# A delta-rule layer on raw keys and queries, its 32x32 systems solved as two 16x16 blocks and a corner made on TensorE

## What is computed

```python
y = b; y = y + w[:, i] * xp[:, i:i + L, :]     # short_conv: 4 taps, then silu on v, unit length on q and k
def step(S, inp):                              # per batch and head, S is 32 x 32
    q_t, k_t, v_t, b_t = inp
    pred = jnp.einsum('bhk,bhkv->bhv', k_t, S)
    S = S + b_t[..., None, None] * (k_t[..., None] * (v_t - pred)[..., None, :])
    o_t = jnp.einsum('bhk,bhkv->bhv', q_t, S)
```

## Time and profile before

| | us |
|---|---|
| median of 3 runs (lowest, highest) | 3324.48 (3321.13, 3328.08) |
| the profiled execution's own time | 3335.67 |
| its span | 3333.9 |
| stage one within it, first output step to last | 0 to about 1325 |
| busy, whole span: TensorE, VectorE, ScalarE, GpSimd | 2692.8, 2510.2, 1182.5, 620.9 |

### The profile page before, as it was taken

One profiled execution on the slowest core, in us unless ns is written; L12 is line 12 of the kernel. 1 busy time (PEld: TensorE's weight loads), 2 busy tenths in 40 slices (PEclk: granted clock), 3 DMA queues, 4 the chain that ended last, 5 costly groups with the idle time before them and its releaser, 6 DMA issues. The chain is left out here.

```text
span 3333.9 us, 88364 instructions
## 1 busy us (share of the span) xinstructions
PE 2692.8 (81%) x35334; PEld 1912.9 (57%) x35356; DVE 2510.2 (75%) x4464; ACT 1182.5 (35%) x2016; POOL 620.9 (19%) x800
## 2 busy tenths in 40 slices
PE   7577777777777755999999995697769999968987
PEld 5455655555555543677777763344456767646664
DVE  6888887888888872477777783887857787834887
ACT  5233333333333320122222221654446565521221
POOL 3232222333322221000000000002600000002343
PEclk9789888888888866999999997899989999988888
DMA  3000000010000101301111112545941212142231
GB/s 88 3 15 28 29 28 29 28 29 28 29 28 29 47 22 64 128 20 51 51 50 50 50 48 89 196 176 179 319 116 51 76 50 76 59 143 83 83 94 51
DMA packets 229643, 234.68 MB, mean 70 GB/s; under 512 B 24112, under 2 KB 157872, under 8 KB 229296
## 3 DMA queue, kind: packets, MB, share of 16 engines
q1 hardware_dynamic: 229296, 229.70, 21.6%
HBM read 136.84 MB, written 92.81 MB: 69 GB/s over the span
## 5 line engine op out<-in xcount | busy, mean ns | idle before, releaser
L1132 PE MATMUL ctxatt_banks<-ctxatt_xT,ctxatt_wq 128*128 128x256 f32 x1024 | 232.9, 381 | 2.9 <-ACT ctxatt_qT L1208 2.1
L1171 PE MATMUL ctxatt_banks<-ctxatt_wo,ctxatt_oT 128*128 128x512 f32 x512 | 230.8, 604 | 4.9 <-DVE ctxatt_norm_y L1277 4.9
L826 DVE TENSOR_TENSOR delta_a<-delta_t_sys 128x30 f32<-128x30 f32 (+14 forms) x480 | 223.3, 465 | 10.3
L849 DVE SCALAR_TENSOR_TENSOR delta_conv<-delta_line,delta_conv_w,delta_conv 128x256 f32<-128x256 f32 x384 | 206.9, 560 | 3.4 <-DVE delta_ss L772 2.1
L829 DVE TENSOR_TENSOR delta_t_sys<-delta_t_sys,delta_a 128x30 f32<-128x30 f32 (+14 forms) x480 | 200.2, 417 | 11.4
L1132 PEld LDWEIGHTS ctxatt_banks<-ctxatt_xT,ctxatt_wq 128*128 128x128 f32 x1024 | 190.0, 191 | 28.7 <-ACT ctxatt_qT L1208 3.3
L393 POOL TENSOR_TENSOR delta_conv<-delta_conv,delta_product 128x256 f32<-128x256 f32 x192 | 148.7, 784 | 263.0 <-ACT delta_product L658 262.7
L508 PE MATMUL delta_banks<-delta_states,delta_kqT 32*32 32x32 f32 x4096 | 60.3, 209 | 154.0 <-DVE delta_states L868 95.2
L489 PE MATMUL delta_banks<-delta_xT,delta_wkT 128*128 128x256 f32 x512 | 135.9, 416 | 43.3 <-ACT delta_beta_T L640 35.8
L656 ACT ACTIVATE delta_conv<-delta_line,delta_conv_b,delta_conv_w 128x256 f32<-128x256 f32 x192 | 115.3, 601 | 153.3 <-POOL delta_conv L393 141.6
L1171 PEld LDWEIGHTS ctxatt_banks<-ctxatt_wo,ctxatt_oT 128*128 128x128 f32 x512 | 96.4, 193 | 117.0 <-issue 110.5
(11 more groups left out here) (328 smaller groups left out, 6728.3 us busy)
## 6 DMA issues: line engine op xcount, KB each, us to landing
h<-ffn_hid SPq DMA_DIRECT2D x66, 256.0 KB, 2.0
ffn_hid<-h SPq DMA_DIRECT2D x6, 1536.0 KB, 13.0
wkv_xT<-xT SPq DMA_DIRECT2D x64, 129.0 KB, 2.8
delta_xT<-xT SPq DMA_DIRECT2D x64, 128.0 KB, 3.0
delta_x<-x SPq DMA_DIRECT2D x16, 512.0 KB, 3.6
xT<-delta_newT SPq DMA_DIRECT2D x64, 128.0 KB, 2.8
x<-delta_new SPq DMA_DIRECT2D x16, 512.0 KB, 3.5
ctxatt_xT<-xT SPq DMA_DIRECT2D x64, 128.0 KB, 2.6
```

What stands on the lines that cost most here:

```text
L826: c.did(dve.tensor_tensor(terms, t_sys[:, j + 1:, j:j + 1].to_broadcast([P, rows, j]), t_sys[:, j:j + 1, 0:j].to_broadcast([P, rows, j]), ...
L849: c.did(dve.scalar_tensor_tensor(to, line[:, i, g, :, j:j + P], conv_w[:, i, g, j:j + 1], to, ALU.mult, ALU.add))
L1132: mm = pe.matmul(b_q[:, i * B * P:(i + 1) * B * P], wq[:, k, pair * P:(pair + 1) * P], xT_sb[:, n.parity, k], start=k == 0, stop=k == KB - 1)
L1171: mm = pe.matmul(b_o[:], oT[:, b, k, :], wo[:, k, :], start=k == 0, stop=k == PAIRS - 1)
```

## The change

Only stage one is edited (the class `ScaledNorm` moves up in the file; a later stage uses it as before).

- Keys and queries stay raw. `kqT` is a copy of the convolution's output by ScalarE (`keep_kq`), no longer turned back by VectorE. The norm of a key enters as `rate` = beta / norm squared (`rate_keys` on GpSimd), into the mask of K K' and into T; that of a query enters through the epsilon of the RMS norm (`q_norm`). `normalise` and `scale_v` are gone.
- All four taps are products on ScalarE, four instructions a projection after the first move (before two); GpSimd adds two of them for a whole third of the projections (`pair_taps`, 128x1024), VectorE adds the rest (`join`, six of 128x1024 a step). `tap` and `add_tap` are gone. silu is one instruction of ScalarE; beta is a tanh and an affine pass.
- A mask is one operation of 128x512 for keys and queries, four a step instead of eight of 128x256.
- The system of 32 is taken as [[T11, 0], [T21, T22]]. `substitute` makes T11 and T22 together, 28 operations instead of 60. Then T21 = T22 (A21 T11): `cross` on TensorE (128 calls of a 32x32 weight with 16 columns), `keep_corner` on ScalarE, `make_corner` on TensorE (128 calls more), `join_corner` on VectorE. `from_systems` has a second transpose (`inverse`). `cross` and `make_corner` use the two banks of `keys_keys`.
- The layer norm's scaling goes from VectorE (`norm.apply`) to ScalarE (`finish`); the outputs' RMS chain has one operation fewer.
- SP issues the stores of t4 ahead of the load of x for t2.
- The order on each list changes; TensorE's is shown in the diff. On GpSimd it is: `scale_t` (t2), `pair_taps` 2 (t1), history 0, `scale_outputs` (t3), `rate_keys` and `mask_beta` (t1), history 1 and 2, bias, `pair_taps` 0 and 1, the norm's root. On VectorE: RMS sum, `turn` 0 and 1, `miss` 0, RMS root, squares, `join_corner`, `join` 4, norms, `join` 5, `turn_outputs`, `turn_beta`, masks 0 and 1, `carry` 0, masks 2 and 3, `to_systems`, `miss` 1, then the 28 operations with the rest between them, `carry` 3, `from_systems`.

The core of the diff:

```diff
+                def pair_taps(n, i):
+                    wait(pool, taps_made, n, TAP_OPS, (i + 1) * MADE)
+                    two_taps, last = slot(n, i)[:, 1], slot(n, i)[:, 2]
+                    pool.tensor_tensor(two_taps, two_taps, last, ALU.add).then_inc(paired, 1)
+
+                def rate_keys(n):
+                    wait(pool, inverted, n, INVERT_OPS, INVERT_OPS)
+                    wait(pool, beta_turned, n, 1, 1)
+                    of_items = rate[:, n.parity].rearrange("p (g x) -> p g x", g=KB)
+                    by_item = beta[:, n.parity, :, 0:KB].rearrange("p x g -> p g x")
+                    pool.tensor_tensor(of_items, r[:, 0].rearrange("p (g x) -> p g x", g=KB), by_item, ALU.mult).then_inc(rated, 1)
 
                 def mask_beta(n):
-                    wait(pool, beta_turned, n, 1, 1)
-                    wait(pool, solved, n, SOLVE_OPS, 0)
+                    wait(pool, rated, n, 1, 1)
+                    wait(pool, masked, n, MASK_OPS, 0)
                     if isinstance(n.index, int) and n.index == 0:
                         pool.wait_ge(loaded, 16 * LOADS)
+                        pool.tensor_copy(weights_kq[:, :, 1], masks[:, 1].unsqueeze(1).to_broadcast([P, ITEMS, DD]))
                     earlier = masks[:, 0].unsqueeze(1).to_broadcast([P, ITEMS, DD])
-                    pool.tensor_tensor(by_group(a_sb[:]), by_group(earlier), beta_of(n), ALU.mult).then_inc(beta_masked, 1)
-
...
-                    pool.tensor_tensor(by_group(tT[:]), by_group(tT[:]), beta_of(n), ALU.mult).then_inc(t_scaled, 1)
+                    wait(pool, joined_corner, n, 1, 1)
+                    pool.tensor_tensor(tT[:], tT[:], rate_of(n), ALU.mult).then_inc(t_scaled, 1)
 
...
+                    if g < 2:
+                        wait(pe, masked, n, MASK_OPS, g - 1)
+                        if g == 1:
+                            wait(pe, joined_corner, n, 1, 0)
+                        else:
+                            wait(pe, corner_kept, n, 1, 0)
+                    else:
+                        wait(pe, masked, n, MASK_OPS, g - 1)
                     cols = b_kk[:, g % 2].rearrange("p (i x) -> p i x", i=QI)
                     pe.sem_inc(passed, 1)
                     for j in range(QI):
...
+                def cross(n):
+                    wait(pe, solved, n, SOLVE_OPS, SOLVE_OPS)
+                    cols = b_kk[:, 0].rearrange("p (i x) -> p i x", i=ITEMS)
+                    pe.sem_inc(passed, 1)
+                    for i in range(ITEMS):
+                        for h in heads():
+                            mm = pe.matmul(cols[h, i], masked_kq[h, n.parity, i, 0], tT[h, i, HALF_DD:], start=True, stop=True)
+                    mm.then_inc(crossed, 1)
+
+                def make_corner(n):
+                    wait(pe, corner_kept, n, 1, 1)
+                    cols = b_kk[:, 1].rearrange("p (i x) -> p i x", i=ITEMS)
+                    pe.sem_inc(passed, 1)
+                    for i in range(ITEMS):
+                        for h in heads():
+                            mm = pe.matmul(cols[h, i], inverse[h, i], corner[h, i], start=True, stop=True)
+                    mm.then_inc(corner_made, 1)
+
...
                             pe.matmul(cols[h, i], kqT[h, n.parity, 1, i], states[h, c, lane], start=True, stop=False)
-                            mm = pe.matmul(cols[h, i], pk[h, n.parity, i, 0], u[h, i], start=False, stop=True)
+                        for h in heads():
+                            mm = pe.matmul(cols[h, i], masked_kq[h, n.parity, i, 1], u[h, i], start=False, stop=True)
                     mm.then_inc(read, 1)
...
+                        cross(t2)
+                    if n:
                         project(n, 2)
                     if t2:
+                        make_corner(t2)
+                    if n:
+                        project(n, 3)
+                    if t1:
+                        keys_keys(t1, 0)
+                        keys_keys(t1, 1)
+                    if t2:
                         update(t2, 0)
                     if n:
-                        project(n, 3)
+                        project(n, 4)
                     if t2:
                         step_state(t2, 0)
+                    if t1:
+                        keys_keys(t1, 2)
+                    if t2:
                         outputs(t2, 0)
-                    if n:
-                        project(n, 4)
+                    if t1:
+                        keys_keys(t1, 3)
+                    if t2:
+                        predict(t2, 1)
+                    if n:
                         project(n, 5)
-                    if t1:
-                        keys_keys(t1, 0)
-                    if t2:
-                        predict(t2, 1)
-                    if t1:
-                        keys_keys(t1, 1)
-                        keys_keys(t1, 2)
-                        keys_keys(t1, 3)
-                    if n:
                         project(n, 6)
                     if t2:
                         update(t2, 1)
...
+                    wait(act, lined, n, len(GROUPS), p)
                     act.activation(conv[:, i, g].rearrange("p (b t) -> p b t", b=B), ln[:, :, 0:P], ACT.Identity,
-                                   bias=conv_b[:, i, g:g + 1], scale=conv_w[:, i, g, 0:1]).then_inc(started, 1)
-                    act.activation(product[:, p % PRODUCTS].rearrange("p (b t) -> p b t", b=B), ln[:, :, 1:1 + P], ACT.Identity,
-                                   scale=conv_w[:, i, g, 1:2]).then_inc(started, 1)
+                                   bias=conv_b[:, i, g:g + 1], scale=conv_w[:, i, g, 0:1]).then_inc(taps_made, 1)
+                    for j in range(1, TAPS):
+                        act.activation(slot(n, i)[:, j - 1, g].rearrange("p (b t) -> p b t", b=B), ln[:, :, j:j + P], ACT.Copy,
+                                       scale=conv_w[:, i, g, j:j + 1]).then_inc(taps_made, 1)
+
+                def keep_kq(n, i):
+                    wait(act, joined, n, JOIN_OPS, 2 * i + 2)
+                    wait(act, read, n, CHUNKS, -CHUNKS)
+                    act.activation(flat(kqT[:, n.parity, i]), conv[:, i].rearrange("p g n -> p (g n)"), ACT.Copy).then_inc(kq_kept, 1)
...
+                def keep_corner(n):
+                    wait(act, crossed, n, 1, 1)
+                    act.activation(flat(corner[:]), b_kk[:, 0], ACT.Copy).then_inc(corner_kept, 1)
+
...
+                def join(n, k):
+                    i = k // 2
+                    total = conv[:, i].rearrange("p g n -> p (g n)")
+                    c = Chain(dve, joined, n, JOIN_OPS)
+                    c.count = k
+                    if k % 2 == 0:
+                        wait(dve, taps_made, n, TAP_OPS, (i + 1) * MADE)
+                    else:
+                        c.settle()
+                        wait(dve, paired, n, 3, i + 1)
+                    c.did(dve.tensor_tensor(total, total, slot(n, i)[:, k % 2].rearrange("p g n -> p (g n)"), ALU.add))
+
...
                     c.link(dve.reciprocal(r[:], root[:]))
                     c.link(dve.tensor_tensor(r[:], r[:], ss[:], ALU.mult))
-                    c.link(dve.tensor_tensor(r[:], r[:], root[:], ALU.add))
-                    c.link(dve.tensor_scalar(r[:], r[:], 0.5, RMS_EPS, ALU.mult, ALU.add))
-                    c.link(dve.reciprocal(r[:], r[:]))
...
-                    c.did(dve.tensor_tensor(pk[:, n.parity, rows, 0], products[:, :, 1], masks[:, 1].unsqueeze(1).to_broadcast([P, QI, DD]), ALU.mult))
+                    dve.tensor_tensor(masked_kq[:, n.parity, rows], products, weights_kq[:, rows], ALU.mult).then_inc(masked, 1)
...
 
-                    Chain(dve, solved, n, SOLVE_OPS).did(dve.memset(t_sys[:].rearrange("p i j -> p (i j)")[:, 0::DD + 1], 1.0))
+                    c = Chain(dve, solved, n, SOLVE_OPS)
+                    c.did(dve.memset(t_sys[:, HALF_DD:, 0:HALF_DD], 0.0))
+                    c.did(dve.memset(t_pad[:, 0:DD * DD][:, 0::DD + 1], 1.0))
 
...
+                    c.count = 2 + k
                     c.settle()
                     j = k // 2 + 1
-                    rows = DD - 1 - j
-                    terms, to = flat(a_sb[:])[:, 0:rows * j].rearrange("p (i c) -> p i c", i=rows), t_sys[:, j + 1:, 0:j]
+                    rows = HALF_DD - 1 - j
+                    parts = flat(squares[:, 0])[:, 0:2 * rows * j].rearrange("p (k i c) -> p k i c", k=2, i=rows)
+                    to, over = blocks[:, :, j + 1:, 0:j], [P, 2, rows, j]
                     if k % 2 == 0:
-                        c.did(dve.tensor_tensor(terms, t_sys[:, j + 1:, j:j + 1].to_broadcast([P, rows, j]),
-                                                t_sys[:, j:j + 1, 0:j].to_broadcast([P, rows, j]), ALU.mult))
+                        c.did(dve.tensor_tensor(parts, blocks[:, :, j + 1:, j:j + 1].to_broadcast(over), blocks[:, :, j:j + 1, 0:j].to_broadcast(over), ALU.mult))
                     else:
```

(24 more changed lines are left out.)

432 lines of the change are left out of this document (203 added, 229 removed).

## The result

The changed kernel takes 3460.42 us (median of four runs, 3459.61 to 3462.79) against 3326.28 for the kernel before on the same chip, a ratio of 1.0407 (95% interval 1.0393 to 1.042). The forecast of 3363 had the right sign and less than a third of the size: 134 us were lost where 39 were expected, and the time lies outside the range.

What follows compares the result with a forecast made beforehand. TensorE, by its instruction supply, was taken to bound stage one; +3.6 us a step gave +47 over thirteen steps, the ends -8, total +39, so a median of 3363 us. Range 3228 to 3425, the forecast's own 3340 to 3400.

Steps and rivals of the forecast that it cites:

- The supply term: TensorE, stage one: 512 added matmuls and loads, in blocks of some 128 every 3.85 us, add 14.3 us a step.
- The first rival: TensorE: supply hides the new blocks, added products cost only their work; step 72.3 us, time 3232; chance 0.25.
- The second: Rival for TensorE: supply cost and saved waits cancel, step stays 77 to 78 us, time 3315 to 3331; chance 0.09.
- Its place: TensorE: most issue stalls fall in cross and make_corner, each lasting 7 us rather than 2.7.
- The waits after: TensorE's semaphore waits: nearly all of 12.2 us a step go, 1.5 come for a new chain, bounds 0 and 4.
- The chain from the corner to the first mask: join_corner, then GpSimd's scale_t to mask_beta, then first mask: 10 us, with keys_keys waiting behind; 1.5 us a step taken.
- beside the rest: ScalarE, rising from 27 to 45 us a step, and GpSimd, falling from 23 to about 18, do not set the end.
- The prediction's own test: Wrong if cross runs 256 matmuls in 3 us, or VectorE or ScalarE delays TensorE over 4 us a step.
- The ends of the stage: Stage one's first and last steps, outside the thirteen full ones: -8 us in sum, bounds -25 and +15.
- the drain: Stage one's end: the step without projections -6 us, the last with a recurrence +8.
- The upper end of the range: The last rival, slower than the forecast: a step of 86 us, time up to 3425; chance 0.12.
- VectorE: Stage one: busy time falls from 66 to 36 to 44 us a step, so VectorE can't be the bound.

Runs made afterwards that it cites:

- e9: e5 with join 5 beside join 4, pair_taps 2 ahead of scale_t, and keep 3 and the first u's copy ahead of ScalarE's gate; 3349.60 us.
- e2: e1 with cross and make_corner cut to one item of 32 (16 matmuls, not 512) and the corner multiplied by zero; 3273.39 us.
- e3: e1 with all 512 corner matmuls kept but one column each instead of 16, corner left out of the result; 3416.70 us.
- e8: The kernel before with stage one's hardware loop written out as straight code; 3310.74 us.
- e10: e9 with stage one's hardware loop written out as straight code; 3318.09 us.
- e1: The changed kernel with one GpSimd call moved: history 0 copied ahead of scale_t and pair_taps 2; 3420.93 us.
- e4: e1 with the whole 32x32 system solved on VectorE in 60 operations, without cross and make_corner; 3300.01 us.
- e6: e4 with ScalarE reordered: keep of projection 0 ahead of the squares, first u's copy ahead of the gate and keep of projection 3; 3261.38 us.
- e7: e6 with stage one's hardware loop written out as straight code; 3209.99 us.
- e5: e1 with join 4 of t1 moved ahead of join_corner on VectorE; 3402.41 us.

## Why the prediction was wrong, step by step

**The supply term was right in its mechanism.** +14.3 us for 512 matmuls and as many loads, from blocks of 128 at 3.85 us, made 79.7 us of own time. After has 80.2, e9 79.7, and e2 without the blocks 66.7. In e3 a sixteenth of the columns brings own time from 80.2 only to 79.3 and the median from 3420.93 to 3416.70.

The blocks can be seen in the DMA queue of instructions. Its lines over eleven steps each of before, e8, after, e10, e1 and e2, in this order (packets, MB, share of 16 engines):

```profile
q8 instruction: 155, 2.54, 1.2%
q8 instruction: 144, 2.36, 1.2%
q8 instruction: 203, 3.33, 1.5%
q8 instruction: 189, 3.10, 1.6%
q8 instruction: 203, 3.33, 1.6%
q8 instruction: 153, 2.51, 1.3%
```

A packet holds 16.4 KB (2.36 MB/144). The two kernels without a loop have one for 254 matmuls and loads (e8 18285 + 18271 over 144, e10 2 x 23978 over 189), so 127 of each; before and after, with the loop, have 1.0 and 1.3 packets more a step for as many matmuls. From e2 to e1 it is 4.5 packets a step more, where the forecast had four blocks. TensorE stops by the same count. In the last step of after that has `cross` and `make_corner`, with no projection beside them:

```profile
1372.16 1.90 PE L543 MATMUL delta_banks<-delta_tT,delta_masked_kq 32*32 32x16 f32 x128 [2.26 <-issue]
1376.45 0.51 PE L543 MATMUL delta_banks<-delta_tT,delta_masked_kq 32*32 32x16 f32 x22 [2.39 <-issue]
...
1381.44 1.90 PE L552 MATMUL delta_banks<-delta_corner,delta_inverse 32*32 32x16 f32 x128 [2.05 <-issue]
1385.19 0.51 PE L552 MATMUL delta_banks<-delta_corner,delta_inverse 32*32 32x16 f32 x22 [1.84 <-issue]
```

128 matmuls pass between two stops, 4.29 and 3.75 us from start to start. And stops and packets go together: in after stops end at 816.93, 820.86 and 824.38, and a packet starts at 818.09, 821.92 and 825.44, 1.1 to 1.2 us behind each, and takes 1.40, 0.98 and 0.88 us. That about one block is held ready fits too: after's list has 384 small matmuls in a row, from step 0 to predict 1, and no stretch of small matmuls in the stage is longer than 256 without a stop. The 3.85 us are a mean and not the best: in e10 two packets start 3.30 us apart (643.06 and 646.36).

The size is less sure than the agreement looks: between split and whole form own time differs by 10.9 (e1, e4), 11.8 (e9, e6) and 11.7 (e10, e7), so that the price is 11 to 13.5 us. The same count for the kernel before gives 60.1, with 3.5 for the loop and 12.2 of waits 75.8, which is 1.8 short of its 77.6; no run shows what the 1.8 are. That 79.7 came out to the tenth in e9 is therefore partly luck. The first rival, that the supply hides the new blocks (0.25), is refuted: it gave a step of 72.3, and even e9, with no waits at all, needs 79.7. The second, that the two cancel, falls with it, since it gave a step of 77 to 78.

**Its place was wrong.** I expected `cross` and `make_corner` to last 7 us each and to hold most of the stalls. Their timeline in after:

```profile
785.01 1.68 PE L543 MATMUL delta_banks<-delta_tT,delta_masked_kq 32*32 32x16 f32 x178
788.65 0.83 PE L543 MATMUL delta_banks<-delta_tT,delta_masked_kq 32*32 32x16 f32 x78 [1.97 <-issue]
789.42 3.42 PE L508 MATMUL delta_banks<-delta_xT,delta_wkT 128*128 128x256 f32 x8
792.77 1.76 PE L552 MATMUL delta_banks<-delta_corner,delta_inverse 32*32 32x16 f32 x169
796.32 1.19 PE L552 MATMUL delta_banks<-delta_corner,delta_inverse 32*32 32x16 f32 x87 [1.79 <-issue]
```

They last 4.5 and 4.7 us (785.01 to 789.48, 792.77 to 797.51) with one stop in the middle. I read this as the work of the projection ahead of each, which lets a block come in: a packet starts at 789.77 and takes 0.93 us, beside the projection from 789.42, and then 169 matmuls of `make_corner` pass without a stop. After the last projection, in the sixteenth system, the two groups do last 8.7 and 7.9 us (from 1368.25 and 1377.75). They hold 36.0 of 143.0 us of issue. Another 38 are the stalls behind the loop's five jumps (4.6 to 5.0 and 2.5 to 3.1 us each), and the rest, 69, lies in the other small products. So a supply bound is paid where the small matmuls stand close, and only for a part where they were added.

**The waits after are the step that failed.** The forecast gave 1.5 us, bounds 0 and 4. After has 6.9 a step. The chain from the corner to the first mask was read for what it leads to, and each station for how long its own instruction takes; what stands behind `scale_t` on GpSimd was not asked. The sentence that ScalarE and GpSimd lie "beside the rest", by busy time, was the error in small: GpSimd is busy for 19.4 us of 87.2 and yet delays all others, by holding 0.20 us of copy behind a wait of up to 40.1. The prediction's own test, "if VectorE or ScalarE is still late for TensorE by over 4 us a step", is what happened, with ScalarE as the messenger. A full step is 9.3 us longer than before's (87.2 against 77.9) where 3.6 were forecast; of the 5.7 between, 5.4 are these waits.

**The ends of the stage.** The forecast had -10 us for the second and third step together (-14 and +4) and +2 for the drain (-6 and +8). The third transpose and the last copy of the stage show both, in one execution of each kernel; before (L812, L664), after (L721) and e9 (L721):

```profile
199.77 2.05 DVE L812 STREAM_TRANSPOSE delta_t_sys<-delta_a 128x1024 f32<-128x1024 f32 x1
...
1320.46 0.60 ACT L664 ACTIVATE delta_newT<-delta_banks 128x512 f32<-128x512 f32 x1 [1.27 <-PE delta_banks L558]
```

```profile
1455.16 0.60 ACT L721 ACTIVATE delta_newT<-delta_banks 128x512 f32<-128x512 f32 x1 [1.27 <-PE delta_banks L603]
```

```profile
1343.55 0.60 ACT L721 ACTIVATE delta_newT<-delta_banks 128x512 f32<-128x512 f32 x1 [1.27 <-PE delta_banks L603]
```

| us against before | forecast | after | e9 |
|---|---|---|---|
| to the third transpose | -10 | +14 | -9 |
| from there thirteen steps | +47 | +111 | +19 |
| from there to the last copy | +2 | +9 | +13 |
| the stage | +39 | +135 | +23 |

So of the 96 us that were missed in the stage, 64 lie in the thirteen steps and 24 ahead of them; e9 takes both away, so that the same missed wait spoiled the first steps too. The drain is a miss of its own, 7 us in after and 11 in e9, which the moves of e9 do not mend. What makes it longer was not tried; the two corner groups of 8.7 and 7.9 us lie in it.

**The sum.** 39 less thirteen times 1.5 of waits is 20 us; e9 lost 20 (3349.60 against 3329.72 beside it). In after, waits and what followed from them were worth 134 - 20 = 114 us, where 20 were allowed. That e9 meets the sum is in part luck: by the table its thirteen steps lost less than the 27 that are left of the forecast without waits, and its drain lost more. Nor is all of the 114 the late corner's doing. e4 has no corner, and moving the copy of `u` there, with the squares, gained 39 us (e6), so a part of the last 55 may be had in any form.

The upper end of the range, 3425 (chance 0.12), came nearest. It had a step of 86 us, 5 over the forecast's, for a mask chain of 4 us and projections at the lower clock (0.5). No run shows this term of 5 us. In its place the runs showed 5.4 us a step more of waits than forecast (6.9 for 1.5), from the queues behind the corner: a longer chain was the right kind, in another place. A slow clock is not shown as a cause: the granted clock is 0.82 in after, 0.85 in e9 and 0.86 in the earlier trace rows, while own time is 80.2 in after and 79.7 in e9.

**VectorE.** The forecast's 36 to 44 us held (41.4). The 28 small operations cost a mean of 0.371 and 0.240 us rather than 0.27; the joins 1.212 each, where L791 gave 1.222:

```profile
L845 DVE TENSOR_TENSOR delta_conv<-delta_conv,delta_product 128x1024 f32<-128x1024 f32 x59 | 71.5, 1212 | 0.0
L908 DVE TENSOR_TENSOR delta_squares<-delta_t_pad 128x28 f32<-128x28 f32 (+6 forms) x140 | 52.0, 371 | 2.8
L910 DVE TENSOR_TENSOR delta_t_pad<-delta_t_pad,delta_squares 128x28 f32<-128x28 f32 (+6 forms) x140 | 33.7, 240 | 2.4
```

## What to carry to other kernels

When a change puts a late result into an in-order queue, list everything behind it in that queue, however short and however idle the engine, and who waits for each; here queue positions cost 114 us of 134. Mend queue positions before judging a change: with its work untouched, this one went from 4.1% slower to 0.7%. And moving work from VectorE to TensorE in small pieces was priced here by the count of instructions, 13.5 us a step for 496 matmuls and as many loads (e1, e2), where a sixteenth of the columns saved 0.9 (e3): the same change without that half and without the loop is 3.5% faster, of which 0.4% is had by writing out the loop of the kernel before.

## What the hardware showed that was not expected

A VectorE operation with two inputs can last as long as the GpSimd operation beside it. Once history stands first (e1, and here e5), the chain of the root comes to lie next to `scale_t` and its followers (VectorE and GpSimd, start us, us):

```profile
1011.42 1.91 POOL L453 TENSOR_TENSOR delta_tT<-delta_tT,delta_rate 128x1024 f32<-128x1024 f32 x1 [25.26 <-DVE delta_tT L925]
1011.84 1.58 DVE L874 TENSOR_TENSOR delta_r<-delta_r,delta_ss 128x64 f32<-128x64 f32 x1
1013.29 2.35 POOL L433 TENSOR_TENSOR delta_product<-delta_product 128x1024 f32<-128x1024 f32 x1
1013.45 2.27 DVE L875 SCALAR_TENSOR_TENSOR delta_r<-delta_r,delta_root 128x64 f32<-128x64 f32 x1
```

L874 ends at 1013.42 and L875 at 1015.72, right after GpSimd's 1013.33 and 1015.64. In after, with GpSimd standing still, they take 0.225 and 0.224 us; in e9, beside GpSimd again, 1.577 and 1.834. So in e9 64 elements cost seven to eight times as much as in after. It cost nothing in the end, since in e9 TensorE waits for nobody. It is not new with the change either. In the kernel before, L826 takes 2.30 us for 108 elements from 281.03, beside GpSimd's L397 (280.77 to 283.21), and in after one L908 a step takes 1.7 to 2.2 us, where half of them take 0.25 or less: that is what lifts its mean to 0.371. Not every operation suffers: in after the joins (L845) take 1.215 us in the median beside GpSimd and 1.221 without it.
